# A graph layer with batch norm: the shift row in fp32 on TensorE for every output part, 20 squared rows from the 14th block on, and late scatters released by 16 of 25 blocks

## The reference

```python
h = jnp.maximum(_layernorm(x, axis=-1), 0.0)
z = jnp.concatenate([h[source], h[target], edge_attrs], axis=-1)
m = jax.nn.sigmoid(z @ W_f + b_f) * jax.nn.softplus(z @ W_s + b_s)
message = jax.ops.segment_sum(m, source, num_segments=100000)
mean = jnp.mean(message, axis=0)
var = jnp.mean((message - mean) ** 2, axis=0)
normed = (message - mean) * jax.lax.rsqrt(var + 1e-5) * gamma + beta
return x + h + normed
```

## Time and profile before

| what | us |
|---|---|
| median of 3 runs | 1061.29 (1059.76 to 1061.81) |
| the profiled execution's own time | 1060.81 |
| span of the profile | 1059.1 |
| busy: TensorE / VectorE / ScalarE / GpSimd | 631.5 / 733.2 / 540.0 / 729.9 |

### The profile page before, as it was taken

The page is one execution under the profiler, slowest core; times in us unless marked ns, Lnnn a source line. Parts: engine busy times, 40 slices in busy tenths (PEclk is TensorE's granted clock), DMA queues, the critical chain, the costliest instruction groups (busy, mean ns, idle before and its releaser), DMA issues.

```text
span 1059.1 us, 11028 instructions
## 1 busy us (share of the span) xinstructions
PE 631.5 (60%) x2458; PEld 453.8 (43%) x2458; DVE 733.2 (69%) x1547; ACT 540.0 (51%) x1181; POOL 729.9 (69%) x652
## 2 busy tenths in 40 slices
PE   0474665666566666656766666676556689944232
PEld 0252444454444444444544454554445578810000
DVE  3884675757575686766777666776666569699788
ACT  1263654545454665545565464655646564434322
POOL 6777878787877877777878777787878752430700
PEclk9855565555555565556555555655656689955555
DMA  8997534343434334333443333433433399799999
GB/s 320 397 394 275 126 96 106 96 106 94 106 94 106 74 86 87 61 81 61 79 87 61 80 71 70 87 63 79 85 56 59 35 380 420 247 302 426 413 404 377
DMA packets 88183, 176.07 MB, mean 166 GB/s; under 512 B 42575, under 2 KB 49299, under 8 KB 79699
## 3 DMA queue, kind: packets, MB, share of 16 engines
q1 hardware_dynamic: 35851, 115.32, 30.9%
q0 software_dynamic: 42880, 20.09, 15.4%
q10 hardware_dynamic: 9416, 40.29, 9.3%
HBM read 107.12 MB, written 68.53 MB: 166 GB/s over the span
## 4 chain that ended last, share of the span: by engine, by line
POOL 48%; DMA 24%; issue 17%; DVE 6%; PE 3%; ACT 1%; SPq 1%; POOLq 0%; ACTq 0%; DVEq 0%
POOL msgs_dram L607 24%; POOL m_buf L594 24%; DMA m_buf<-msgs_dram 8%; DMA msgs_dram<-y_kept 8%; DMA msgs_dram<-sums,target 6%; PE ps_all L1544 2%; DVE m_buf L1795 2%; DMA out_dram<-m_buf 2%; DVE m_buf L1801 1%; DVE sums L1717 1%; PE ps_all L1539 0%; SPq L499 0%; POOL m_buf L617 0%; DVE target L794 0%; DVE m_buf L763 0%
## 5 line engine op out<-in xcount | busy, mean ns | idle before, releaser
L594 POOL DMA_INDIRECT m_buf<-in_x_dram,m_buf x384 | 366.9, 955 | 118.7 <-issue 109.4
L607 POOL DMA_INDIRECT msgs_dram<-sums,target x184 | 289.7, 1574 | 56.2 <-issue 55.8
L1171 PE MATMUL ps_all<-sums,m_last 128*128 128x64 f32 x920 | 188.5, 394 | 124.8 <-ACT m_last L1033 107.1
L1171 PEld LDWEIGHTS ps_all<-sums,m_last 128*128 128x128 f32 x920 | 181.0, 303 | 136.2 <-issue 112.5
L719 DVE TENSOR_REDUCE m_last<-late 128x24 f32<-128x1536 f32 (+1 forms) x49 | 85.3, 1742 | 87.8 <-ACT late L984 87.8
L1131 PE MATMUL ps_all<-ident,m_buf 128*128 128x128 f32 x192 | 53.0, 431 | 128.6 <-DVE m_buf L809 128.6
L1145 PEld LDWEIGHTS ps_all<-m_buf 128*128 128x128 f32 x392 | 91.9, 322 | 49.0 <-issue 49.0
L794 DVE TENSOR_TENSOR target<-moved,m_last 128x4 int32<-128x4 f32 x49 | 9.6, 196 | 146.1 <-POOLq L605 145.8
L1033 ACT ACTIVATE m_last<-m_last,one_col 128x512 f32<-128x512 f32 x196 | 107.6, 550 | 1.6
L1131 PEld LDWEIGHTS ps_all<-ident,m_buf 128*128 128x128 f32 x192 | 34.9, 217 | 160.4 <-DVE m_buf L809 138.5
L1143 PE MATMUL ps_all<-m_buf 128*128 128x512 f32 x98 | 98.8, 1111 | 0.0
(11 more groups left out here) (171 smaller groups left out, 1078.1 us busy)
## 6 DMA issues: line engine op xcount, KB each, us to landing
m_buf<-msgs_dram SPq DMA_DIRECT2D x38, 1024.0 KB, 11.9
m_buf<-in_x_dram SPq DMA_DIRECT2D x48, 512.0 KB, 5.0
msgs_dram<-y_kept SPq DMA_DIRECT2D x14, 1536.0 KB, 11.0
out_dram<-m_buf ACTq DMA_DIRECT2D x20, 1024.0 KB, 11.2
m_buf<-src_rows_dram SPq DMA_DIRECT2D x47, 256.0 KB, 4.1
y_spill_dram<-y_kept ACTq DMA_DIRECT2D x19, 512.0 KB
y_kept<-y_spill_dram SPq DMA_DIRECT2D x8, 1024.0 KB, 12.1
m_buf<-in_x_dram,m_buf POOLq DMA_INDIRECT x392, 2.5
```

The source lines that it names most:

```text
L594: pool.indirect_dma_start(xg[:, n % G_SLOTS, 2 * j + c, :], None, x, bass.IndirectOffsetOnAxis(ap=ids[:, c, n * TILES + j:n * TILES + j + ...
L607: pool.indirect_dma_start(msgs, bass.IndirectOffsetOnAxis(ap=target[:, n % UNROLL, j:j + 1], axis=0), comb[:, n % COMB_SLOTS, j, :], None, ...
L1171: pe.matmul(ps_c[:, j, :], same_of(b, j, j + 1)[:, 0, :], msg_of(g)[:, b, :], start=(b == 0 and not begun), stop=(b == j), skip_group_chec ...
```

## The change

- `add_row` loses its arguments: every part gets the shift row as one fp32 matmul for 8 rows (`ones[0:1, :]` with `shift[0:1, :]`), after `shift_ready`. `take_mean` and its six subtractions, `split_shift` and the adding of beta during the scan are gone. VectorE computes `shift` ahead of the parts, and waits for `block_crossed` before it scales a held block.
- Blocks 13 to 23 have 20 of 32 rows squared by ScalarE (16, and 12 in blocks 22 and 23, before); the three banks are used from block 15 on instead of block 19.
- GpSimd works out a list `late_add` of targets, in which rows of held blocks are replaced by rows behind the table (`dump_row`, `dump_late`). The late scatters take this list, and wait for the blocks before the held ones (0 to 15), for the rest rows and for the list, not for all blocks.

```diff
@@ -79,10 +79,10 @@
 SQ_ROWS = 20
 SQ_BESIDE = 18
 BESIDE = range(4, 13)
-SQ_THEN_ROWS = 16
+SQ_THEN_ROWS = 20
 SQ_FIRST = (6, 2)
 SQ_THEN = (6, 4, 5)
-SQ_CHANGE = 19
+SQ_CHANGE = 15
 Y_ROWS = 32
 BANK_ROWS = 8
 PSUM_BANKS = 8
@@ -92,9 +92,6 @@
 FINISH_AT = 13
 CORRECT_AT = 15
 WHOLE = 1.5 * 2.0 ** 23
-BETA_PARTS = Y_FIRST + 2
-FEW_SQUARED = 2
-FEW_ROWS = 12
 LAST_PIECES = ((0, 16, 8), (16, 8, 0), (24, 5, 5))
 SPLIT = 3
 
@@ -314,6 +311,7 @@
     moved = keep("moved", [P, TILES])
     dump_late = keep("dump_late", [P, LATE - 1, TILES])
     later_late = keep("later_late", [P, LATE - 1, TILES])
+    at.dump_row, at.dump_late = dump_row, dump_late
     in_next = keep("in_next", [P, TILES])
     in_last = keep("in_last", [P, LATE - 1, TILES])
 
@@ -1237,15 +1235,14 @@
     sq_tail = sums(F)
     m_rest = sums(F)[0:N_REST, :]
     corr_row = keep("corr_row", [P, F])
-    left = sq_acc[:, 0:SPLIT, :]
-    part = keep("part", [P, SPLIT, F], BF16)
-    shift_row = keep("shift_row", [P, F], BF16)
     late_node = keep("late_node", [P, LATE_TILES])
     marked = keep("marked", [P, LATE_TILES])
     late_q = keep("late_q", [P, LATE_TILES])
     late_row = keep("late_row", [P, LATE_TILES])
     in_range = keep("in_range", [P, LATE_TILES])
     spare_row = keep("spare_row", [P, LATE_TILES])
+    late_add = keep("late_add", [P, LATE_TILES], I32)
+    to_dump = keep("to_dump", [P, LATE_TILES])
 
     last_bank = (PSUM_BANKS - 1) * BANK_ROWS
     ps_gram = ps_all[:, last_bank:last_bank + 2, :].rearrange("p r f -> p (r f)")
@@ -1269,9 +1266,6 @@
     rstd_ready = sem("rstd_ready")
     chain = sem("chain")
     shift_ready = sem("shift_ready")
-    split_steps = sem("split_steps")
-    split_done = sem("split_done")
-    mean_taken = sem("mean_taken")
     scale_ready = sem("scale_ready")
     scaled = sem("scaled")
     y_copied = sem("y_copied")
@@ -1282,6 +1276,8 @@
     rest_stored = sem("rest_stored")
     list_steps = sem("list_steps")
     list_done = sem("list_done")
+    add_steps = sem("add_steps")
+    add_listed = sem("add_listed")
     spare_listed = sem("spare_listed")
     late_added = sem("late_added")
     late_scaled = sem("late_scaled")
@@ -1307,8 +1303,6 @@
         n = BLOCKS[b][1]
         if b == NB - 1:
             return list(LAST_PIECES)
-        if b >= NB - 1 - FEW_SQUARED:
-            return [(0, n, FEW_ROWS)]
         return [(0, n, n * (SQ_ROWS if b < BESIDE.start else SQ_BESIDE if b in BESIDE else SQ_THEN_ROWS) // S_BLK)]
 
     def wait_piece(eng, b, j):
@@ -1530,13 +1524,14 @@
         def clear(bank):
             return clear_bank(pe, at, bank)
 
-        def add_row(k, weights, row):
+        def add_row(k):
 
             _, _, n = y_parts[k]
             pe.wait_ge(y_copied, k + 1)
             for c in range(0, n, BANK_ROWS):
                 w = min(BANK_ROWS, n - c)
-                ins = pe.matmul(ps_y(k)[:, c:c + w, :], weights, row.unsqueeze(1).to_broadcast([row.shape[0], w, F]),
+                ins = pe.matmul(ps_y(k)[:, c:c + w, :], ones[0:1, :],
+                                shift[0:1, :].unsqueeze(1).to_broadcast([1, w, F]),
                                 start=False, stop=True, skip_group_check=True)
             ins.then_inc(y_summed, 1)
 
@@ -1571,9 +1566,6 @@
                 for bank in sorted(set(range(PSUM_BANKS - 1)) - set(SQ_FIRST)):
                     ins = clear(bank)
                 ins.then_inc(banks_blank, 1)
-            if Y_BLOCK < b <= Y_BLOCK + Y_FIRST:
-                pe.wait_ge(affine_loaded, 32)
-                add_row(b - Y_BLOCK - 1, ones[0:1, :], bet[0:1, :])
             if b == M_BUFS:
                 pe.wait_ge(rest_loaded, 16)
                 cross(m_rest[:, :], F, False)
@@ -1589,11 +1581,9 @@
         pe.matmul(ps_tot, ones[:, :], sq_tail[:, :], start=False, stop=True).then_inc(total_ready, 1)
         pe.wait_ge(var_ready, 1)
         clear(PSUM_BANKS - 1).then_inc(banks_blank, 1)
-        for k in range(Y_FIRST, BETA_PARTS):
-            add_row(k, ones[0:1, :], bet[0:1, :])
-        pe.wait_ge(split_done, 1)
-        for k in range(BETA_PARTS, len(y_parts)):
-            add_row(k, ones_b[:, :], shift_row[0:SPLIT, :])
+        pe.wait_ge(shift_ready, 1)
+        for k in range(len(y_parts)):
+            add_row(k)
 
     def gpsimd(pool):
 
@@ -1635,6 +1625,18 @@
                                ).then_inc(list_steps, 1)
             pool.wait_ge(list_steps, 8)
             pool.tensor_tensor(late_row[:, :], late_row[:, :], in_range[:, :], ALU.mult).then_inc(list_steps, 1)
+            for k in range(LATE):
+                of_k = slice(k * TILES, (k + 1) * TILES)
+                ins = pool.tensor_tensor(to_dump[:, of_k], at.dump_late[:, k - 1, :] if k else at.dump_row[:, :],
+                                         late_node[:, of_k], ALU.subtract)
+            ins.then_inc(add_steps, 1)
+            pool.wait_ge(list_steps, 9)
+            pool.wait_ge(add_steps, 1)
+            pool.tensor_tensor(to_dump[:, :], to_dump[:, :], late_row[:, :], ALU.mult).then_inc(add_steps, 1)
+            pool.wait_ge(add_steps, 2)
+            pool.tensor_tensor(to_dump[:, :], to_dump[:, :], late_node[:, :], ALU.add).then_inc(add_steps, 1)
+            pool.wait_ge(add_steps, 3)
+            pool.tensor_copy(late_add[:, :], to_dump[:, :]).then_inc(add_listed, 1)
             pool.tensor_tensor(late_node[:, :], late_node[:, :], spare_row[:, :], ALU.subtract
                                ).then_inc(list_steps, 1)
             pool.wait_ge(list_steps, 10)
@@ -1651,17 +1653,16 @@
         pool.wait_ge(spare_listed, 1)
         correct()
         list_targets()
-        for b in range(M_BUFS):
-            pool.wait_ge(m_loaded[b], 16 * len([k for k in range(NB - 1) if scan_buf(k) == b]))
-        for loaded in last_loaded:
-            pool.wait_ge(loaded, 16)
+        for b in range(SCAN_BUFS):
+            pool.wait_ge(m_loaded[b], 16 * len([k for k in range(held[0]) if scan_buf(k) == b]))
         pool.wait_ge(rest_loaded, 16)
+        pool.wait_ge(add_listed, 1)
 
         def add_late(k):
 
             for j in range(TILES):
                 pool.indirect_dma_start(
-                    msgs, bass.IndirectOffsetOnAxis(ap=target[:, (EARLY + k) % UNROLL, j:j + 1], axis=0),
+                    msgs, bass.IndirectOffsetOnAxis(ap=late_add[:, k * TILES + j:k * TILES + j + 1], axis=0),
                     late_comb[:, k * TILES + j, :], None, compute_op=ALU.add,
                 ).then_inc(late_added, 16)
 
@@ -1693,15 +1694,6 @@
             dve.tensor_scalar(mean[:, :], msg_sum[:, :], 1.0 / NODES, None, ALU.mult).then_inc(chain, 1)
             dve.wait_ge(chain, 1)
             dve.tensor_tensor(mean2[:, :], mean[:, :], mean[:, :], ALU.mult).then_inc(chain, 1)
-
-        def take_mean(k):
-
-            i, r, n = y_parts[k]
-            m = m_out(i, r, n)
-            dve.wait_ge(rows_squared, chunks_of(order[i]))
-            dve.wait_ge(block_crossed, order[i] + 1)
-            dve.tensor_tensor(m, m, mean[:, :].unsqueeze(1).to_broadcast([P, n, F]), ALU.subtract
-                              ).then_inc(mean_taken, 1)
 
         def correct():
 
@@ -1742,8 +1734,6 @@
                 take_means()
             elif b == CORRECT_AT:
                 correct()
-            if order[0] + 2 <= b < order[0] + 2 + BETA_PARTS:
-                take_mean(b - order[0] - 2)
         dve.wait_ge(rows_added, last_piece)
         dve.tensor_reduce(sq_row[:, :], sq_acc[:, :, :].rearrange("p r f -> p f r"), AX.X,
                           ALU.add).then_inc(acc_reduced, 1)
@@ -1765,37 +1755,15 @@
         dve.tensor_tensor(scale[:, :], var[:, :], gam[:, :], ALU.mult).then_inc(scale_ready, 1)
         dve.wait_ge(scale_ready, 1)
         dve.tensor_tensor(mean2[:, :], mean[:, :], scale[:, :], ALU.mult).then_inc(chain, 1)
-        dve.wait_ge(mean_taken, BETA_PARTS)
-
-        def split_shift():
-
-            dve.wait_ge(shift_ready, 1)
-            for k in range(SPLIT):
-                dve.tensor_copy(part[:, k, :], shift[:, :] if k == 0 else left[:, k, :]).then_inc(split_steps, 1)
-                dve.wait_ge(split_steps, 1 + 2 * k)
-                if k < SPLIT - 1:
-                    dve.tensor_tensor(left[:, k + 1, :], shift[:, :] if k == 0 else left[:, k, :], part[:, k, :],
-                                      ALU.subtract).then_inc(split_steps, 1)
-                    dve.wait_ge(split_steps, 2 + 2 * k)
-            for k in range(SPLIT):
-                if k == 0:
-                    ins = dve.tensor_scalar(shift_row[:, :], part[:, k, :], ident[:, k:k + 1], None, ALU.mult)
-                else:
-                    ins = dve.scalar_tensor_tensor(out=shift_row[:, :], in0=part[:, k, :], scalar=ident[:, k:k + 1],
-                                                   in1=shift_row[:, :], op0=ALU.mult, op1=ALU.add)
-                ins.then_inc(split_done if k == SPLIT - 1 else split_steps, 1)
-                if k < SPLIT - 1:
```

(10 more changed lines are left out.)

## The result

The changed kernel takes 1102.16 us in the median (1101.11 to 1102.3), the kernel before 1061.15 in the same runs: ratio 1.0386, 95% interval 1.0368 to 1.0404, so 41 us slower. Forecast were 1098.0 us and a range of 1088 to 1107. The profiled execution has a span of 1100.4 us (forecast 1095.8).

A forecast was written before the change was run, and what follows sets the result against it. TensorE was to bound the output: start at 923.6 us plus 167.0 us of matmuls gives 1090.6, plus 5.2 us of end a span of 1095.8; the profiled execution 1097.5, the median 1098.0 us, range 1088 to 1107.

The forecast's parts named there:

- The price of the one-row matmul: Output: each one-row fp32 matmul costs TensorE 1.71 us at clock 0.50; 98 of them, one shorter, take 167.0 us.
- Rival (a): Output: clock granted at 1.00, TensorE hidden, DMA and VectorE bound, 1056 us; chance 0.08, shared with a case of unmoved scatters.
- (b): Output: clock granted part of the time, a matmul 1.42 us at half and half, about 1070 us; chance 0.06.
- (c): Output: each matmul costs more, as 1.87 us with 128 rows, or the PSUM ring stalls; 1113 us; chance 0.05.
- the ring of two halves: Output: two PSUM halves; VectorE's addition and ScalarE's copy take 4.6 us while TensorE works 6.84, so no stall.
- the engine with most room in the output: Output before the change, 939 to 1046 us: TensorE was said to have most room, busy only 41 us.
- The start of the run: Start of the output: variance at 921.9 us, shift ready at 923.5, TensorE's matmuls begin at 923.6 us.
- the prediction's own sign (a variance after 926 us): End of the scan: a variance after 926 us, instead of near 922, would show the scan's step wrong.
- its step on the end of the scan: Scan's end: fewer products free TensorE, VectorE becomes the bound at 920.0 us, variance at 921.9 us, 3.6 us earlier.
- The end: End of the output: 5.2 us from the start of the last addition to the span's end, at 1095.8 us.
- The scatters: Late scatters: first at about 904.5 us instead of 914.43, SP's reloads go on at about 933 instead of 943.27.

## Why the prediction was right, and where it was off

**The price of the one-row matmul.** 98 matmuls (one of them shorter) at 1.71 us were put at 167.0 us; the changed kernel shows 166.98. That the clock mattered, and that it stays at 0.50 with one row, is now shown: with 128 rows the same matmuls run at 1.00 and the loss of 41 us shrinks to 4. The rule of the Trainium skill that was set against it (page TensorE: Matmul & The Clock Gate, the section on the HAM clock gate: sustained matmul activity releases the throttle) fits the run with 128 rows, whose clock rose from 0.50 to 1.00 between 935.5 and 936 us, when TensorE had been busy since 931.04; it does not fit 167 us of one-row matmuls without a gap at 0.50. The measurement decides.

Part of the call was luck. The prediction took the price from four matmuls whose clock was 0.50 from 927.5 us to their end at 931.66, 4.2 us; the matmuls of 128 rows also stayed at 0.50 for more than 4.4 us (to 935.5) before their clock rose, so the stretch in rows 7 and 8 was too short to show that it would not rise. Only its fall in the midst of one-row work (1.00 at 926, 0.50 at 927.5 us) spoke for that, and that the number of rows decides was not in the prediction.

Rival (a) is out by the measurement, and so are (b), since no stretch of the run has another clock than 0.50, and (c), since the matmul kept its price and the ring of two halves never held TensorE. Two prices of the rivals were off as well: (c) took 1.87 us for a fp32 matmul of 128 rows at 0.50, where they cost 1.71 with 128 rows too; and (a) put the kernel with a granted clock at 1056 us, faster than before, where the run with 128 rows, at 1.00 for most of its output, takes 1064.79; only with the squared rows of before does it come to such a time (1056.65). The prediction also called TensorE the engine with most room in the output; ScalarE (38.08 us) and GpSimd (21.78) had more.

**The start of the run** was mis-sized: 923.6 us was forecast, 929.57 came. The variance was not 3.6 us earlier but 2.3 later (927.84 against 925.54). By the prediction's own sign (a variance after 926 us) its step on the end of the scan was wrong, in direction too: the squared rows cost time (5.5 us alone) where they were thought to save it, and the time still fell into the range of 1088 to 1107 us because that is wide enough for a start 6 us late.

```profile
900.53 2.00 DVE L1709 TENSOR_TENSOR sums<-sums,ps_all 128x512 f32<-128x512 f32 x3
...
924.00 1.03 DVE L1738 TENSOR_REDUCE sums<-sums 128x64 f32<-128x512 f32 x1
...
927.84 0.22 DVE L1751 SCALAR_TENSOR_TENSOR sums<-ps_all,sums 128x64 f32<-128x64 f32 x1 [2.22 <-PE ps_all L1581]
```

Three terms of that step's sum were too small. Block 14's first addition was put at 897.2 us and began at 900.53 (3.3 us): 1.1 us of it is that this execution entered the scan later (SP's first load at 846.42 instead of 845.34 us), the rest is the wait for the third chunk of block 13, as the run with 16 rows there shows. From there to the end of the reduction I had 22.8 us, and it took 24.5 (900.53 to 925.03), as the chunks of block 15 waited 0.6 us for ScalarE and a block of three chunks took about 2.1 us instead of 1.96. And from there to the variance I had taken 1.89 us from before, where it took 2.81: the profile shows the clock falling in 925 to 926 us (0.60 there, 0.50 after), after TensorE, which had ended its products at 920.6, had waited 4.81 us for VectorE.

```profile
925.00:926.00 1.00, 0.63 (x3) 0.66 (x4) 0.62 (x3) 0.03 (x1) 1.00 (x1) 0.60 0.31 24
926.00:927.00 1.00, 1.00 (x7) 1.00 (x6) 0.00 (x0) 0.00 (x0) 0.70 (x2) 0.50 0.96 147
```

That VectorE would be the bound of the scan's end was right. **The end** was 1.4 us shorter than the 5.2 us taken from the earlier trace rows, as the last addition begins at 1096.65 us and the span ends at 1100.4. That fits DMA engines with less to do (a share of 0.53 from 1046 us to the end, against 0.85 before), but no run separates it. Start (+6.0) and end (-1.4) give the 4.6 us by which the span missed.

**The scatters** moved as forecast, though later, as the list hangs on the same small operations: the first at 907.66 us instead of 904.5. The gate behind them did not open the reloads at about 933 us, as the prediction had it, but at 947.68 us, later than the 943.27 before: the last of the spilled parts of x + h stands ahead of them in SP's queue, and went out at 947.2 us, when ScalarE's copy of that part's place (945.33 + 1.88 us) was done, a copy that goes at the pace of TensorE's parts. It cost nothing, as VectorE never waited for a reload in the output. In the kernel before, the scatters bring nothing either, where I had left them up to 3 us.

**The parts of the loss.** Alone, the shift costs 32 us, the squares 5.5, the scatters 0. Their sum, 38, is near the 41 of the whole; the difference fits the reading that with TensorE as the bound every microsecond of a later start counts in full: TensorE starts 7.0 us later in the changed kernel than with the shift alone (929.57 against 922.53, 0.9 of it ahead of the scan), and the spans differ by 7.4 (the medians by 8.9).

## What to carry to other kernels

Before an operation is called hidden on an engine with room, multiply its price at the clock that this very form of it runs at by its count: 98 matmuls that took 97 us, mostly at the full clock, were hidden in an output of 124 us, and 167 us at half of it were not. The four matmuls already in the trace gave the price at 0.50, though not how long the clock would stay there. Adding a constant row with all 128 rows (the row divided by 128) instead of one cost the same 0.855 us a record at 0.50, and here it let the clock rise. When work is moved from one engine to another at the end of a stage, look at what else waits behind the added piece on every engine in between: a chunk of 0.42 us cost 2.6. And when a gate in a queue opens earlier, look at what stands next to it in the same queue before counting the gain.

## What the runs showed of the hardware

TensorE without a gap for 167 us on one-row fp32 matmuls stayed at 1.2 GHz throughout, while matmuls of 128 rows, at the same 0.855 us a record while at 1.2 GHz, rose to 2.4 GHz and kept it over 945 to 999 us with gaps of 0.7 to 1.3 us between groups of 3.4 to 3.7 us. And small operations of VectorE (128x4 and 128x64) lasted 1.3 to 1.8 us when they fell beside GpSimd's two additions of 128x768 (1.80 us each), against 0.16 to 0.25 us alone, in the kernel before, the changed one and the run with 16 rows alike; each ended with GpSimd's addition, and a reduction from PSUM beside one was not slowed (0.41 us).
